# VectorE's order in the softmax passes of a graph kernel: the message product ahead of the preceding step's scale-and-add pairs

## The reference

```python
xw = (x @ W).reshape(n_nodes, H, C)
al_s = einsum('nhc,hc->nh', xw, a_src); al_d = einsum('nhc,hc->nh', xw, a_dst)
logits = leaky_relu(al_s[src] + al_d[dst], 0.2)
m = segment_max(logits, dst)
e = exp(logits - m[dst])
denom = segment_sum(e, dst)
out = segment_sum((e / denom[dst])[:, :, None] * xw[src], dst)
```

## Time and profile before

| | us |
|---|---|
| median of 3 runs | 11693.11 |
| lowest, highest | 11682.03, 11700.05 |
| profiled execution, its own time | 11695.19 |
| its span in the trace | 11693.4 |
| message product, busy in 342 instructions | 681.4 |
| scale (L1783) and add (L1787), busy in 684 each | 258.2, 263.2 |
| gathers of the softmax passes, busy in 2736 | 2593.8 |

### The profile page before, as it was taken

One profiled execution on the slowest core, in us unless ns is written; L12 is line 12 of the kernel. 1 busy time (PEld: TensorE's weight loads), 2 busy tenths in 40 slices (PEclk: granted clock), 3 DMA queues, 4 the chain that ended last, 5 costly groups with the idle time before them and its releaser, 6 DMA issues. The chain is left out here.

```text
span 11693.4 us, 143529 instructions
## 1 busy us (share of the span) xinstructions
PE 6135.8 (52%) x40035; PEld 4863.7 (42%) x40036; DVE 4364.6 (37%) x13034; ACT 1969.3 (17%) x5277; POOL 6088.9 (52%) x6396
## 2 busy tenths in 40 slices
PE   3545455555544345565556556655555555555454
PEld 3444444555322223343434344444344444444444
DVE  4333322222211113555555455554444444433233
ACT  1222210100211112111112111111211111111111
POOL 4666656666466663444443444444355555355554
PEclk6565655555676766666667566666655555556666
DMA  4444422222222232333332333333223333233333
GB/s 124 141 141 139 138 69 78 79 77 70 68 73 74 73 75 77 107 106 107 107 106 80 111 107 106 105 106 107 63 79 80 79 79 79 63 97 96 94 97 83
DMA packets 774630, 1092.81 MB, mean 93 GB/s; under 512 B 389184, under 2 KB 429440, under 8 KB 774160
## 3 DMA queue, kind: packets, MB, share of 16 engines
q0 software_dynamic: 233760, 503.07, 17.2%
q1 hardware_dynamic: 540784, 588.70, 17.0%
HBM read 1016.16 MB, written 75.04 MB: 93 GB/s over the span
## 5 line engine op out<-in xcount | busy, mean ns | idle before, releaser
L681 POOL DMA_INDIRECT gat_rows<-xw_table,gat_index x2736 | 2593.8, 948 | 2958.4 <-DVE gat_msg_s L1763 1822.8
L1850 PE MATMUL bank<-gat_msg_s,gat_hot 128*128 128x264 f32 (+1 forms) x5472 | 2077.5, 542 | 680.9 <-DVE gat_msg_s L1763 438.8
L1850 PEld LDWEIGHTS bank<-gat_msg_s,gat_hot 128*128 128x128 f32 x5472 | 1443.5, 301 | 1138.9 <-issue 905.6
L681 POOL DMA_INDIRECT att_rows<-pre_table,att_index x912 | 862.6, 946 | 814.0 <-ACT att_index L671 518.2
L681 POOL DMA_INDIRECT msg_rows<-pre_table,msg_index x912 | 865.1, 949 | 639.3 <-ACT msg_index L671 371.2
L681 POOL DMA_INDIRECT gcn_rows<-in_x,gcn_index x912 | 878.0, 963 | 564.1 <-ACT gcn_index L671 284.0
L893 PE MATMUL bank<-gcn_rel,gcn_rhot 100*128 100x64 f32 x3648 | 701.6, 344 | 890.0 <-issue 698.0
L681 POOL DMA_INDIRECT gcn_rows<-x_table,gcn_index x912 | 885.8, 971 | 542.3 <-issue 278.6
L893 PEld LDWEIGHTS bank<-gcn_rel,gcn_rhot 100*128 100x128 f32 x3648 | 678.9, 269 | 928.5 <-issue 862.7
L730 PE MATMUL bank<-gcn_msg_s,gcn_hot 128*128 128x128 f32 x3648 | 814.6, 374 | 448.8 <-issue 441.8
L730 PEld LDWEIGHTS bank<-gcn_msg_s,gcn_hot 128*128 128x128 f32 x3648 | 707.1, 277 | 512.5 <-issue 512.0
(11 more groups left out here) (285 smaller groups left out, 10049.3 us busy)
## 6 DMA issues: line engine op xcount, KB each, us to landing
gcn_ids<-rel_rows SPq DMA_DIRECT2D x228, 400.0 KB
gat_hot_half<-edge_hots SPq DMA_DIRECT2D x342, 256.0 KB
gat_dhot<-dst_hots SPq DMA_DIRECT2D x342, 256.0 KB
gcn_dst<-dst_rows SPq DMA_DIRECT2D x114, 512.0 KB
gat_rows<-xw_table,gat_index POOLq DMA_INDIRECT x2736
edge_hots<-gcn_hot_half SPq DMA_DIRECT2D x114, 256.0 KB
dst_hots<-gcn_dhot SPq DMA_DIRECT2D x114, 256.0 KB
gcn_hot_half<-edge_hots SPq DMA_DIRECT2D x114, 256.0 KB
```

The costliest lines, as they stand in the source:

```text
L681: pool.indirect_dma_start(self.rows[n.q][:, j, :], None, self.table, bass.IndirectOffsetOnAxis(ap=self.index[n.q][:, j:j + 1], axis=0))\
L1850: ins = pe.matmul(sum_ps[g][:, 0:wide], hot[n.q][:, g * GROUP + j, :], msg[q][:, g * GROUP + j, :], start=j == 0, stop=j == GROUP - 1)
```

## The change

In VectorE's order of `gat_pass`, `messages` of step t - 2 moves from between the two scale-and-add pairs of step t - 3 to ahead of both. Nothing else is different.

```diff
@@ -1797,8 +1797,8 @@
                 dve.sem_inc(topped, 1)
                 dve.sem_inc(added, PAIR)
                 dve.sem_inc(fade_kept, TWO)
-                pipeline(dve, (1, scan), (2, maxima), (1, run_ends), (1, cut_ends), (2, logits), (2, keep_fade), (3, add(0)),
-                         (2, messages), (3, add(1)))
+                pipeline(dve, (1, scan), (2, maxima), (1, run_ends), (1, cut_ends), (2, logits), (2, keep_fade), (2, messages),
+                         (3, add(0)), (3, add(1)))
```

## The result

| | us |
|---|---|
| kernel before, median of 14 | 11694.69 |
| changed kernel, median of 14 (11714.56 to 11736.24) | 11722.65 |
| ratio, 95% interval | 1.0025 (1.0017 to 1.0033) |
| profiled execution of the changed kernel, its own time | 11736.24 |

The account below looks back on a forecast made before the run. The order of waits, clocked by the gathers' end, was taken to bound the kernel. Passes 1 and 2 +64 -61, third +55 -12, disturbed pairs -13, ends +3: +36 us on 11693, given as 11728 us; range 11540 to 11800.

Parts of the forecast that it names:

- The ring: Softmax passes: logits L1750, product, next gathers, then L1750 released after the last gather; a long first-pass step sums to 16.07 us.
- the block products' start: TensorE's L1840, feeding L1750: starts 3.56 or 4.34 us after the first gather's start, by when L1744 is ready.
- The rival of a fixed time: Block products take a fixed time, so VectorE and TensorE form the ring: +0.31 us a step, 11786 us, chance 0.17.
- the rival of a growing lag: Already late steps' wait from last gather to L1750 jumps another 1.4 us: 11946 us, half of them 11840; chance 0.07.
- The product earlier: VectorE's message product starts 1.04 us after L1750 instead of 1.60 or 1.33: gains 0.56 us a step, third pass 0.29.
- What stands behind it: TensorE's sums and VectorE's work after the product come 0.87 us later (third pass 0.6); nothing charged for the first gather.
- ordinary steps: Undisturbed softmax steps: passes 1 and 2 +64 and -61 us, third pass +55 and -12 us.
- pairs around the stops: Nine step pairs per pass disturbed by VectorE stopping up to 13.5 us at L1787; each still gains: -13 us.
- ends: Nine end steps without gathers become longer by about 0.3 us: +3 us.
- nothing to be seen: Rival: a quarter to half of the short lags after the last gather survive: 11670 to 11716 us, chance 0.12.
- short-lag step: Step where L1750 starts 0.2 us after the last gather, not 1.6: 14.65 us in the first pass, forecast to become 15.51.
- my first rival: Lag from last gather to L1750 stays, set by place in the four-step turn or TensorE's state: 11551 us, chance 0.28.

Follow-up runs that it names:

- e10: Kernel before with 6 gathers instead of 8 in each step of the softmax passes, output wrong: 10826.77 against 11695.65 us, ratio 0.9255.
- e9: Kernel before with both scale-and-add pairs moved ahead of the logits, on a chip with late release: 11873.32 against 11875.22 us, ratio 1.0002.
- e7: Kernel before plus two scratch VectorE instructions (0.9 us) behind each message product, on a chip with late release: 11882.33 against 11875.22 us, ratio 1.0008.
- e1: Kernel before plus two scratch VectorE instructions (0.9 us) behind each message product, on a chip without late release: 8817.78 against 8729.88 us, ratio 1.010.
- e4: Kernel before with 8 block products instead of 24 a step (coarser logits), on the chip without late release: 8723.49 against 8729.88 us, ratio 0.9995.
- e12: Kernel before with only the first add pair moved ahead of the logits, so the product comes early: 11726.15 against 11695.65 us, ratio 1.0025.
- e11: The changed kernel repeated against the kernel before: 11720.44 against 11695.65 us, ratio 1.0024.
- e6: The kernel before, unchanged, traced on another chip with late release: 11880.53 us (one execution) against 11875.22.
- e8: Kernel before with only the first add pair moved ahead of the logits, on a chip with late release: 11845.92 against 11875.22 us, ratio 0.9973.
- e5: The changed kernel against the kernel before on a third chip, with late release: 11809.68 against 11929.4 us, ratio 0.9903.
- e2: Kernel before with only the first add pair moved ahead of the logits, on the chip without late release: 8724.38 against 8729.88 us, ratio 0.9995.

## Why the prediction was right, and which step of it was not

**The ring.** Right, and now shown: L1750 goes with the end of the gathers (e10), to within one or two of TensorE's pauses, not at a fixed time after the block products' start (4.4 to 4.6 us in e10, 6.1 to 6.5 in the changed kernel, 8.3 to 8.5 in e9, means of a pass) nor with what VectorE does behind the product (e7). The rival of a fixed time is out. The Trainium skill ("Perfetto Trace Analysis", "Per-engine timelines") has the semaphore wait for PSUM's acknowledgement: in e1 that and all else is over 0.03 us after the drawn end. On the other chips no run tells whether the acknowledgement, the products or the signal is what comes late, as said under e1 to e4. Out is also the rival of a growing lag: at distances up to 6.0 us it is 1.65 to 1.71.

**The product earlier.** Right. 1.10 us after L1750 instead of the forecast 1.04; the hand-over from ScalarE to VectorE takes 0.10 us, not 0.05. The wait shows as L1763 behind L1675, 285 times.

**What stands behind it.** L1850 waits for the adds in L1787 more than 300 times, as forecast, and e12 beside e11 shows that nobody is late by it. The first gather, now beside the adds, takes 0.94 us (5186.14 above), as beside an idle VectorE: nothing was to be charged. The warning of the Trainium skill ("SBUF — State Buffer", "SBUF: two separate sides") did not bear on these adds.

**The sum.** By parts, from the starts of the product in the two first traces:

| | forecast | measured |
|---|---|---|
| ordinary steps, passes 1 and 2 | 64 - 61 = +3 | 14.9 + 8.6 - 5.7 = +17.8 |
| ordinary steps, pass 3 | 55 - 12 = +43 | 41.3 - 1.1 = +40.2 |
| pairs around the stops | -13 | -11.1 - 11.6 - 1.7 = -24.4 |
| ends | +3 | +4.0 |
| sum | +36 | +37.6 |

(-5.7 and -1.1 are the first nine steps of the passes.) Two terms were mis-sized and cancel. The step is 15.59 us, not 15.51 (0.06 from the product's start, the rest from the lag): 182 x 0.08 = 15 us. And the pairs around the stops win 1.2 to 1.3 us on average in the first two passes, not 0.56. That average hides what happened: one stop of the first pass is missing (4.7 us), the last pair of each pass wins 3.2 and 3.3, one of the second 2.5, and the other fourteen 0.1 to 1.1. The stops of 13.5 us are shorter too, 8.0 to 11.2 us, but that alone wins little: at the stop below VectorE waits 11.14 instead of 13.52 us, and its pair takes 34.3 instead of 34.5.

```profile
5160.78 0.43 DVE L1787 TENSOR_TENSOR acc<-acc,bank 128x264 f32 x1 [11.14 <-remote]
```

Why a stop is missing or shorter stays open. Two smaller slips in the sums: 11693 + 36 is 11729, and the rival "nothing to be seen" is mispriced. A survivor is worth 0.86 + 0.56 = 1.42 us, in the third pass 1.3 + 0.27, 172 us for all 117, so a quarter to half of them gives 11686 to 11643 us, not 11716 to 11670; and the break-even with the kernel before lies at about 2 survivors in 10.

**The step that failed.** "L1744 would come 3.56 + 0.87 = 4.4 us after the first gather in what was a short-lag step, just where the long lag of 1.62 stands now (4.34)." The lags went as forecast, in all 240 steps, but the reason doesn't carry them: they are lost without it as well. e12 leaves L1744 at 3.2 to 4.8 us and loses them as well, at the same cost within 6 us; e9 puts it at 2.4 to 4.1 us and has them no more; e6 has the distances of the kernel before, and 20 short lags instead of 115. What holds in every trace is the other half: with a distance of 3.7 us or more no lag is under 0.6. Below 3.7 it is under 0.6 in 115 of 132 steps of the kernel before, but in 20 of 132 of e6, 6 of 130 of e12, 4 of 238 of e9 and none of 131 of e8. So an early L1744 goes with every short lag and is far from enough for one. That both repeat with the turn of four steps, as my first rival had pointed out, may be why they stood together in the kernel before. That rival (the lag stays, 11551 us) is out as well, though: it wanted them to survive the earlier product.

**What sets the lag** stays open. Short lags were seen in numbers in the unchanged kernel only, on one chip in 48% of the steps and on another in 8%, and each of four edits (time behind the product, the product earlier with or without the adds moved, two gathers fewer) left few or none. The lags lie 0.7 to 0.8 us apart because the release keeps to the 0.716 us of TensorE's pauses, as said under e1 to e4. What makes TensorE pause, and what decides after how many pauses the release comes, no run tests. A phase between these pauses and the ring, that any edit upsets, would fit. So on this reading, which is argued and not shown, the change pays for lost luck: it takes 0.5 and 0.24 us off each step, and gives back 1.4 to 1.5 us in the nearly half of them that had the short lag. The forecast was right in the number of lags lost, and that was partly luck. On the chip of e5, the kernel before probably has few such lags to lose (it takes 235 us more), or has the stops that the changed kernel lacks there, or both, and the change wins 1%; this is argued from e6, where the time lies between the two, and no trace of the kernel before was taken there.

**A better version.** None for all chips. e2's order gains 0.27% where the kernel before takes 11.88 ms, loses 0.25% where it takes 11.70 and is level where it takes 8.73. Fewer gathers with more rows each would attack the term that all runs agree on; this was not tried.

## What to carry to other kernels

When a wait is let go at one of a few fixed distances from an event of another engine, find by an experiment what picks the distance before you price an edit by it, and look whether another engine's starts keep to the same spacing: two quantities that alternate with the same loop look like cause and effect in every trace of the one kernel. Price such an edit by its worst value for all steps (here 15.6 us a step in the first two passes), since the favourable one may be a coincidence that any edit undoes. And with effects of 0.3%, compare on more than one chip: the same change measured +0.25% and -1.0%.

## What the runs showed of the hardware

- What waits for a group of TensorE's small products can be let go late while GpSimd issues indirect gathers: L1750 started 6.1 to 8.5 us after the block products (means of a pass, eight gathers) and 0.1 to 2.0 us after the last gather (in 5 steps up to 1.2 us before its end), wherever the kernel before took 11.69 to 11.93 ms, and 0.03 us after their end on the chip where it took 8730 us. With it goes a step of 15.6 (e12) against 10.0 us (e2) of the same kernel. The pick products behind them start over 2.9 to 5.2 us there instead of 0.6; TensorE's single turns are signalled on time (0.01 us).
- The lags are bunched around 0.3, 1.0 and 1.8 us rather than spread (e6: 20, 37 and 183 steps), 0.7 to 0.8 us apart, like the starts of TensorE's products behind its pauses (0.70 to 0.73 us); with six gathers they all are 1.2 to 1.6.
- Where the release is late the size differs from one comparison to the next: the changed kernel's lag is 1.65 us in two and 1.81 in a third.
- Of the 18 stops of the first two passes (one every twelve steps, 96 gathers) all are there in the first trace and in e12, 17 in that of the changed kernel and 2 in e5. In e6 to e9, at one place, it is 16 in e6 and 1 in e7, so their number goes with the kernel's order too. GpSimd pauses after each 96 gathers (2.81 us between two starts instead of 1.25) in all of these, also where VectorE doesn't stop. With six gathers a step the steps stay at 13.3 us throughout the first two passes, without any.
